# Bucket sums of a graph kernel on one core: message rows become the stationary operand, the one-hot matrix the moving one, and the own nodes enter through a diagonal matrix

## The reference, cut to what matters

```python
def reference(x, src, dst, edge_weight, ...):
    xn = layernorm(x)
    msgs = edge_weight[:, None] * xn[dst]
    agg = segment_sum(msgs, src, num_segments=n)      # 12500 sums of 256 features
    h = (1.0 + eps) * xn + agg                        # own node and the sum of its messages
    h = bn_relu(h @ W1 + b1, g1, be1)
    h = bn_relu(h @ W2 + b2, g2, be2)
    x = x + h
    xf = layernorm(x)
    H = gelu(xf @ Wf + bf)
    probs = softmax(H @ Wg + bg)                      # 8 experts, the best one is taken
    return x + probs[best] * (H @ Wd[best] + bd[best])
```

## Time and profile before

| | us |
|---|---|
| median of 3 runs (lowest, highest) | 3958.41 (3956.34, 3971.75) |
| the profiled execution's own time | 3961.0 |
| its span, first to last instruction | 3959.2 |
| TensorE busy with matmuls | 3311.6 (84% of the span) |
| VectorE busy | 2474.8 (63%) |
| mean granted TensorE clock | 0.936 of full speed |
| message rows read, each bucket | 1300 KB and 1170 KB |

### The profile page before, as it was taken

One profiled execution on the slowest core, in us unless ns is written; L12 is line 12 of the kernel. 1 busy time (PEld: TensorE's weight loads), 2 busy tenths in 40 slices (PEclk: granted clock), 3 DMA queues, 4 the chain that ended last, 5 costly groups with the idle time before them and its releaser, 6 DMA issues. The chain is left out here.

```text
span 3959.2 us, 80107 instructions
## 1 busy us (share of the span) xinstructions
PE 3311.6 (84%) x23786; PEld 2806.0 (71%) x23787; DVE 2474.8 (63%) x6083; ACT 1364.0 (34%) x2175; POOL 711.5 (18%) x705
## 2 busy tenths in 40 slices
PE   0097688868888888888999999989688888839998
PEld 0096466658777777777888888864367666639998
DVE  5865322236766666756777777743477777766665
ACT  2200155535555555550000000015455454453332
POOL 0000000005555455550000000000012222212222
PEclk9999988878988888899999999999899999969999
DMA  3800000017777777778999999940023334346665
GB/s 131 287 0 0 0 0 0 0 31 281 297 283 285 276 287 289 290 279 311 331 332 328 333 330 333 329 144 0 27 102 139 149 144 149 121 183 210 211 209 154
DMA packets 214698, 750.83 MB, mean 190 GB/s; under 512 B 28411, under 2 KB 64549, under 8 KB 189430
## 3 DMA queue, kind: packets, MB, share of 16 engines
q1 hardware_dynamic: 130694, 446.18, 33.3%
q0 software_dynamic: 83952, 304.02, 19.7%
HBM read 411.44 MB, written 353.16 MB: 193 GB/s over the span
## 5 line engine op out<-in xcount | busy, mean ns | idle before, releaser
L1218 PE MATMUL coll_ps_sum<-coll_rows,coll_hot 128*128 128x256 f32 x3724 | 823.8, 380 | 20.7 <-DVE coll_hot L1159 20.7
L1218 PEld LDWEIGHTS coll_ps_sum<-coll_rows,coll_hot 128*128 128x128 f32 x3724 | 700.9, 191 | 114.7 <-DVE coll_hot L1159 22.2
L1159 DVE TENSOR_SCALAR coll_hot<-coll_nodes,coll_rows 128x128 f32<-128x128 f32 x1862 | 495.0, 344 | 228.5 <-PE coll_ps_sum L1218 160.5
L920 PE MATMUL send_ps_msg<-send_window,send_pick 128*128 128x256 f32 x3584 | 587.2, 317 | 18.4 <-ACT send_msg L953 12.0
L953 ACT ACTIVATE send_msg<-send_ps_msg 128x1024 f32<-128x1024 f32 x448 | 454.2, 1024 | 320.9 <-PE send_ps_msg L920 208.5
L920 PEld LDWEIGHTS send_ps_msg<-send_window,send_pick 128*128 128x128 f32 x3584 | 511.8, 215 | 50.5 <-ACT send_msg L953 18.0
L801 POOL DMA_INDIRECT messages<-send_msg,send_to x448 | 468.0, 1045 | 432.9 <-ACT send_msg L953 298.7
L844 DVE TENSOR_SCALAR send_pick<-send_ps_local,edges_down 128x1024 fp32r<-128x1024 f32 x224 | 287.6, 1284 | 263.6 <-PE send_ps_local L907 215.1
L703 ACT ACTIVATE rank_only<-rank_ranks 98x1024 f16<-98x1024 f32 x224 | 204.6, 917 | 472.6 <-PE rank_ranks L669 472.4
L1251 ACT ACTIVATE nodes_hid<-coll_ps_turned 128x256 f32 (+1 forms) x98 | 37.5, 383 | 813.4 <-PE coll_ps_turned L1063 813.4
L633 DVE TENSOR_TENSOR rank_hot<-edges_bucket,edges_of_bucket 128x1386 bf16<-128x1386 bf16 x112 | 98.7, 882 | 284.1 <-PE rank_ranks L669 283.8
(11 more groups left out here) (292 smaller groups left out, 5758.6 us busy)
## 6 DMA issues: line engine op xcount, KB each, us to landing
coll_rows<-messages SPq DMA_DIRECT2D x98, 1300.0 KB, 7.6
coll_rows<-messages SPq DMA_DIRECT2D x98, 1170.0 KB, 7.6
exp_pay<-regions SPq DMA_DIRECT2D x105, 646.0 KB
send_window<-node_table SPq DMA_DIRECT2D x112, 256.0 KB
node_table<-prep_both SPq DMA_DIRECT2D x25, 1024.0 KB, 4.7
coll_own<-node_table SPq DMA_DIRECT2D x98, 256.0 KB, 4.8
prep_xt<-in_x_dram SPq DMA_DIRECT2D x24, 512.0 KB, 4.8
gate_xt<-in_x_dram SPq DMA_DIRECT2D x24, 384.0 KB
```

The lines of the kernel that those rows point to most:

```text
L920: ins = pe.matmul(ps_msg[:, q % 2, a, :], pick[:, q * RUN + a, :], window[:, s, part * D:(part + 1) * D], start=(part == 0), stop=(part == 1))
L1159: ins = dve.tensor_scalar(hot[:, j, :], nodes[:], rows[:, s, j, ROW_ID:ROW_ID + 1], rows[:, s, j, ROW_W:ROW_W + 1], ALU.is_equal, ALU.mult)
L1218: ins = pe.matmul(ps_sum[:, s, 0:D], hot[:, j, :], rows[:, s, j, 0:D], start=(j == 0), stop=(j == CJ - 1))
```

## The change

The operands are exchanged. For each tile j and each half f of the features, a 128x128 piece of the message rows is now the stationary operand, and the one-hot matrix (128 columns) the moving one. The sum comes out as features by nodes, in a PSUM bank for each f, so nothing has to be turned. The own node is added by four more matmuls a bucket, whose stationary operand is a 128x128 piece of `own` (rounded part and remainder, two feature halves) and whose moving one is `eye`, the identity times 1+eps, built once. `own_sum`, `turn_sums`, `finish` and `turn` go from the fast path; `sums_ready` and `turned` go with them. TensorE waits at a bucket's first half for `kept` (ScalarE's copy) of b-2, and at the second half for `own_in`. ScalarE copies straight from the sums behind `added`. The load of `own` no longer waits for `sums_ready`.

```diff
+        eye = m.sb("eye", [P, P])
+        ps_sums = m.ps("ps_sums", [P, 2, DH, 512])
+        ps_sum = ps_sums[:, 0]
@@ sync
-                    if later(b, 2):
-                        sp.wait_ge(sums_ready, b - 1)
                     sp.dma_start(own[:, s, :], table[ds(b * P, P), :]).then_inc(own_in[s], 16)
@@ vector
-                def finish(b, s, uses):
-                    dve.wait_ge(added, 2 * b + 2)
-                    if later(b, 1):
-                        dve.wait_ge(sums_ready, b)
-                    dve.wait_ge(own_in[s], 16 * uses)
-                    if later(b, 2):
-                        dve.wait_ge(turned, b - 1)
-                    dve.sem_inc(dve_turn, 1)
-                    own_sum(dve, steps, s, s, ps_sum[:, s, 0:D]).then_inc(sums_ready, 1)
+                dve.tensor_scalar(eye[:], c.ident[:], c.eps1[:, 0:1], None, ALU.mult).then_inc(eye_ready, 1)
...
-                    if later(b, 1):
-                        finish(b - 1, 1 - s, 2 * i + (u - 1) // 2 + 1)
@@ tensor
-                def turn(b, s):
-                    pe.wait_ge(sums_ready, b + 1)
-                    if later(b, 2):
-                        pe.wait_ge(kept, b - 1)
-                    turn_sums(pe, s).then_inc(turned, 1)
                         pe.wait_ge(hot_ready, 2 * b + h + 1)
                         if h == 0 and later(b, 2):
-                            pe.wait_ge(sums_ready, b - 1)
+                            pe.wait_ge(kept, b - 1)
+                        if h == 1:
+                            pe.wait_ge(own_in[s], 16 * (2 * i + u // 2 + 1))
+                            for f in range(DH):
+                                for q in range(2):
+                                    pe.matmul(ps_sums[:, s, f, 0:P], own[:, s, q * D + f * P:q * D + (f + 1) * P], eye[:],
+                                              start=False, stop=False)
                         for j in range(j0, j1):
-                            ins = pe.matmul(ps_sum[:, s, 0:D], hot[:, j, :], rows[:, s, j, 0:D],
-                                            start=(j == 0), stop=(j == CJ - 1))
+                            for f in range(DH):
+                                ins = pe.matmul(ps_sums[:, s, f, 0:P], rows[:, s, j, f * P:(f + 1) * P], hot[:, j, :],
+                                                start=(j == 0), stop=(j == CJ - 1))
                         ins.then_inc(added, 1)
-                        if h == 0 and later(b, 1):
-                            turn(b - 1, 1 - s)
@@ scalar
-                    act.wait_ge(turned, b + 1)
+                    act.wait_ge(added, 2 * b + 2)
                     act.sem_inc(act_turn, 1)
-                    act.activation(place(i, u), turned_sums(u % 2), ACT.Copy).then_inc(kept, 1)
+                    act.activation(place(i, u), ps_sums[:, u % 2, :, 0:P], ACT.Copy).then_inc(kept, 1)
```

More of the change, by code:

```diff
@@ L1005, in collect @@
         gathered = rows[:].rearrange("p s j f -> p (s j f)")[:, 0:GT * 2 * D].rearrange("p (t f) -> p t f", t=GT)
-        ps_sum = m.ps("ps_sum", [P, 2, 512])
+        eye = m.sb("eye", [P, P])
+        ps_sums = m.ps("ps_sums", [P, 2, DH, 512])
+        ps_sum = ps_sums[:, 0]
         ps_turned = m.ps("ps_turned", [P, 2, 512])
@@ L1012, in collect @@
         added = m.sem("added")
-        sums_ready = m.sem("sums_ready")
-        turned = m.sem("turned")
+        eye_ready = m.sem("eye_ready")
         kept = m.sem("kept")
@@ L1198, in _ @@
                     all_buckets(dve, bucket)
-                    finish(NBK - 1, (NBK - 1) % 2, (NBK - 1) // 2 + 1)
             @block.tensor
@@ L1240, in _ @@
                 with pe.Else():
+                    pe.wait_ge(eye_ready, 1)
                     all_buckets(pe, bucket)
-                    turn(NBK - 1, (NBK - 1) % 2)
             @block.scalar
```

## The result

The changed kernel takes 4048.8 us (4040.3 to 4054.1, 4 runs) against 3957.4 us before (4 runs); these medians lie 91.4 us apart. Worked out from all runs, the changed kernel takes 1.0218 times as long, with a 95% interval of 1.0198 to 1.0237, that is +86 us, 79 to 94. Forecast were 4053 us and +95 us. The profiled executions took 4054.1 and 3961.0 us, with spans of 4052.3 and 3959.2 us, 93.1 us apart.

What follows compares the result with a forecast made beforehand. TensorE's load-and-matmul pairs were taken to bound `collect`: 84 pairs at 0.112 us add 0.99 us a bucket, +97 us over 98 buckets, less 1.6 us at the end, so +95 us to 4053 us; range 4024 to 4124 us.

Steps and rivals of the forecast that it cites:

- What binds: In `collect`, TensorE's gapless pairs set the stage: 8.42 us a bucket before, times 98 buckets.
- The number of pairs: TensorE per bucket: 76 tile pairs plus 8 own pairs, 84 in place of 38 and two transpositions.
- The pace: Start-to-start time of plain float32 pairs with 128 loaded and 128 moving columns: 0.112 us, range 0.109 to 0.120.
- fp32r surplus: Extra pair time seen in fp32r rows, 0.120 us at 256 columns; the forecast took plain float32 to have none.
- The rival at 0.120: TensorE pairs in `collect` take 0.120 us as the load's surplus returns: +161 us, 4120 us; chance 22%.
- The sum: TensorE in `collect`: 84 x 0.112 = 9.41 us a bucket, 0.99 more than 8.42; times 98, +97 us.
- the 1.6 us of the end: After the last matmul, VectorE instructions and transpositions go, so ScalarE starts earlier: -1.6 us, once.
- The own node: Own matmuls on TensorE in place of the transpositions: 8 x 0.112 - 0.21 = 0.69 us a bucket.
- VectorE, ScalarE, `own_in`, `kept`: Other engines' work and the moved waits in `collect` cost nothing inside the stage; VectorE's wait for TensorE grows about 190 us.
- The transfers: DMA in `collect`: bytes stay, 7.7 us of full rate fits inside 9.4 us a bucket; share near 0.81.
- the floor of 7.7 us: Full-rate DMA time a bucket, from share 0.91 of 8.42 us; taken to set the end if TensorE were faster.
- The rival on the faster side: Pairs in `collect` paced below 0.100 us, DMA setting the end: -76 us, 3882 us; no change or gain 7%.

Runs made afterwards that it cites:

- e1: Changed kernel without its four own-node matmuls a bucket (sums lack the own node); 3785.4 us against 3781.4 before, ratio 1.0011.
- e2: Changed kernel with the two own parts added on VectorE first, leaving 4 own pairs of 8 a bucket; ratio to before 1.0131.
- e7: Kernel before, operand order and transpositions kept, with the own node entering by two 256-column matmuls a bucket; 4043.6 us, ratio 1.0218.
- e8: Changed kernel with loads of 64 columns in place of 128, without e4's GpSimd memset; ratio to before 1.0189.
- e11: Repeat of e9 (changed kernel in fp32r, moving operands streamed twice) beside e10 and e12 on one chip; ratio to before 0.9535.
- e6: Kernel before with rows and one-hot matrix in fp32r, one pair a matmul, own node still added by VectorE; 3899.8 us, ratio 0.9851.
- e10: e6 with the moving message features streamed twice, 512 columns in place of 256; ratio to before 0.9839.
- e5: Changed kernel with rows, one-hot matrix, own rows and diagonal in fp32r, one pair a matmul; 4006.3 us, ratio to before 1.0124.
- e3: Changed kernel with 64 moving columns in place of 128 in all matmuls of the stage; 4708 us, ratio to before 1.2452.
- e9: e5 with every moving operand streamed twice, 256 columns in place of 128; 3608.8 us, ratio to before 0.9542.
- e12: Repeat of e6 (kernel before in fp32r) beside e10 and e11 on one chip; ratio to before 0.9826.
- e4: Changed kernel with loads of 64 columns in place of 128, features left out zeroed by a GpSimd memset; ratio to before 1.0231.

## Why the prediction was right

- *What binds.* TensorE's pairs set the stage before and after, with no gap inside a bucket. Shown by the windows and by e1, e2, e7 and e8, whose buckets (8.49, 8.93, 9.29, 9.17 us, in that order) are within 0.01 us of pairs times pace.
- *The number of pairs.* 84 a bucket, as counted.
- *The pace.* 0.112 forecast, 0.1117 measured. The step that chose it held: plain float32 has no fp32r surplus, and the load ends last by a hair (e8). The rival at 0.120 fell. The Trainium skill, "TensorE: Matmul & The Clock Gate", section on the back-to-back issue gap, gives some 81 ns a matmul at 128 columns; the trace gives 112 ns for float32, and the measurement decides. Its section on LDWEIGHTS puts the load at columns / 1.2, 107 ns; measured is a pace 5 ns longer, small for one and 84 x 98 times here.
- *The sum.* 0.99 us a bucket forecast, 0.96 measured in one steady bucket; most of the difference is 84 pairs at 0.3 ns less. On average it is 0.945, since a bucket before took 8.435 us and not the 8.42 read from one. 98 x 0.945 less the 1.6 us of the end, which came as forecast, is the stage's +91.0 us. The profiled span is +93.1, the medians +91.4, all runs together +86 (79 to 94), so the forecast of +95 lies just above what was measured.
- *The own node* is the loss: forecast 0.69 of 0.99 us a bucket. By e1 it is 9.38 - 8.49 = 0.89 us for its 8 pairs, against 0.21 for the transpositions: 0.68; the exchange costs 8.49 - 8.21 = 0.28, forecast 0.30.
- *VectorE, ScalarE, `own_in`, `kept`.* All hidden, as forecast. VectorE's waits for TensorE grew by 226 us (160.5 to 386.1), not 190. The forecast left out its waits for the rows: they went from 65.5 to 4.1 us, since the transfers now have 9.4 us a bucket, and came back as waits for TensorE. All its idle time before the one-hot tiles grew by 172.5 us (228.5 to 401.0).
- *The transfers.* This step was wrong, though nothing hung on it in the forecast. The DMA share was forecast at 0.81 and is 0.85, and the floor of 7.7 us, share times bucket, is not a floor: e11 moves a bucket's rows in 6.7 us, at 418 GB/s, on a faster chip, and e6 on the slower one reaches 419 GB/s from 1795 to 1800 us. The rival on the faster side was priced by it, and could have been worth more had its pace come true.

## What to carry to other kernels

Where TensorE binds in plain float32, count its pairs of load and matmul and take each at the longer of load and stream (0.1117 and 0.1092 us here); exchanging the operands keeps the streamed columns and can double the loads, and work that another engine did beside TensorE at no cost in time (two VectorE instructions) cost 0.89 us a bucket here as four small matmuls. Removing a stall or an engine's step off the path shows no gain until the bound is gone: the same exchange was 2.2% slower in plain float32 and 3% faster than the old order in fp32r with a clock near full (e11 against e10). Before halving the passes or columns of a loop, look what becomes of the granted clock: half the work took nearly the same time a bucket (e5, 8.96 us against 9.38) or twice as long (e3, 84 x 0.213 = 17.9 us), until the moving operand was streamed twice (e9), which gave the fastest kernel of all, 0.954 of before, in the shorter number type.

## What the runs showed of the hardware that was not expected

The granted clock, at 0.50 when the stage began behind an idle TensorE, stayed there for the whole stage in e3 and e5, though TensorE was never without work: a pair there streamed 64 plain float32 or 128 fp32r columns under a load of 128. It rose to 1.00 in the changed kernel and in e9, whose pairs stream 128 plain float32 or 256 fp32r columns, and stayed there in e9 through idle time of 93 in 500 us. The columns of a pair are not all of it: e12 streams 256 fp32r columns a pair as e9 does, has TensorE busy for 324 of 500 us, and its clock is 0.51; with 512 columns it is 0.93 (e10). What exactly decides was not shown. The Trainium skill, "TensorE: Matmul & The Clock Gate", section on HAM oscillation, names idle gaps as what takes the clock down. These traces agree that it is low behind a long gap (18.7 us in e5, 27.8 us in e3) and that gaps of about 1 us in e9 don't bring it down; that it stays low under work without a gap, as in e3 and e5, that section does not cover.

At the lower clock the load is slower too, 333 ns in place of 192 (e3), so that a load-paced pair takes 0.213 us in place of 0.112.

Beside a memset of GpSimd over 21.43 us a VectorE instruction of 0.16 us took 20.83 us (e4); without the memset it took 0.16 us again (e8). The same kernel took 3957 us on one chip and 3782 us on others. The difference lies ahead of `collect`, whose first matmul starts at 1797 us in the changed kernel and at 1615.5 us in e8; the pairs in it are paced alike (e1).
